# Fewer TensorE signals and fewer GpSimd waits in a two-layer graph network kernel

## The reference, cut to what matters

```
# layer 0
msgs   = x[dst] @ Wd + x[src] @ Ws + edge_weight[:, None] * ww + bm
agg    = segment_max(msgs, dst);  agg = where(deg > 0, agg, 0)
x1     = layernorm(x + relu(x @ W1a + agg @ W1b + b1) @ W2 + b2)
# layer 1
h      = x1 @ node_fc_W + node_fc_b
a      = sum(h[src] * h[dst], -1)                         # one number an edge
t      = relu((edge_attr @ edge_fc_W + edge_fc_b) @ rel_att_W1[m] + rel_att_b1[m])   # m = 0, 1, 2
g      = sigmoid(sum(t * rel_att_W2[m], -1) + rel_att_b2[m])
alpha  = segment_softmax(a, dst);  beta = segment_softmax(g, dst)
h_att  = segment_sum(alpha * (h[src] @ sum_k node_att_W[k])) / 3
h_rel  = segment_sum(sum_m beta[:, m] * (h[src] @ rel_att_W[m])) / 3
h_red  = relu(concat(h_att, h_rel) @ out_fc_W + out_fc_b)
out    = layernorm(x1 + gate * where(deg > 0, h_red, h) + (1 - gate) * x1)
```

## Time and profile before

| | |
|---|---|
| median of 3 runs | 2891.07 us (2887.76 to 2893.6) |
| the profiled execution | 2877.64 us, span 2875.9 us |
| busy share of the span | PE 65%, PEld 40%, DVE 46%, ACT 39%, POOL 59% |
| mean granted clock of TensorE | 0.786 of full speed |
| phase_runs, first to last gather | 73.7 to 1254.7 us |
| phase_nodes0, first gather to last product | 1291.9 to 1408.8 us |
| phase_edges, first gather to last window added | 1412.5 to 2745 us |
| gathers | 784 in phase_runs, 57 in phase_nodes0, 784 in phase_edges |

### The profile page before, as it was taken

One profiled execution on the slowest core, in us unless ns is written; L12 is line 12 of the kernel. 1 busy time (PEld: TensorE's weight loads), 2 busy tenths in 40 slices (PEclk: granted clock), 3 DMA queues, 4 the chain that ended last, 5 costly groups with the idle time before them and its releaser, 6 DMA issues. The chain is left out here.

```text
span 2875.9 us, 42972 instructions
## 1 busy us (share of the span) xinstructions
PE 1864.3 (65%) x9844; PEld 1144.2 (40%) x9844; DVE 1326.2 (46%) x5218; ACT 1107.7 (39%) x3259; POOL 1686.3 (59%) x1718
## 2 busy tenths in 40 slices
PE   4467777767667676455556666666666666666764
PEld 3112222222222222114445555555555555555663
DVE  3455444444433434323434444444444444444567
ACT  1133333333333333233454444444444444444533
POOL 1666666666776777636355555555555555555434
PEclk7688888888888888787767777778777777777786
DMA  5443333333333233322311121111111111111122
GB/s 179 153 177 104 119 105 119 104 119 104 119 103 99 100 115 114 106 75 81 108 44 51 46 51 49 48 49 51 45 51 50 47 49 51 49 47 51 46 68 69
DMA packets 115920, 238.36 MB, mean 83 GB/s; under 512 B 32905, under 2 KB 68422, under 8 KB 106102
## 3 DMA queue, kind: packets, MB, share of 16 engines
q0 software_dynamic: 52832, 109.39, 14.3%
q1 hardware_dynamic: 56458, 100.52, 9.5%
q10 hardware_dynamic: 6540, 27.42, 2.8%
HBM read 169.22 MB, written 67.89 MB: 82 GB/s over the span
## 5 line engine op out<-in xcount | busy, mean ns | idle before, releaser
L402 POOL DMA_INDIRECT d_region<-d_h,d_region x784 | 749.5, 956 | 556.0 <-issue 307.7
L515 POOL DMA_INDIRECT acc<-d_src_product,b_region x784 | 810.3, 1033 | 404.5 <-issue 215.3
L596 PE MATMUL banks<-acc,b_region 64*128 64x512 f32 x1176 | 367.5, 732 | 375.8 <-issue 166.5
L1500 DVE TENSOR_TENSOR acc<-acc,banks 128x160 f32 x784 | 252.6, 322 | 278.1 <-issue 82.8
L596 PEld LDWEIGHTS banks<-acc,b_region 64*128 64x128 f32 x1176 | 109.0, 211 | 583.4 <-issue 307.8
L804 DVE SCALAR_TENSOR_TENSOR acc<-b_region,acc 128x128 f32<-128x128 f32 x784 | 270.8, 346 | 124.7 <-DMA acc<-d_src_product,b_region 107.5
L701 ACT ACTIVATE gate_col<-banks,b_region 128x1024 f32<-128x1024 f32 x147 | 161.4, 1113 | 391.4 <-remote 273.9
L1296 PE MATMUL banks<-d_region 128*128 128x128 f32 x1568 | 297.5, 349 | 2.8 <-issue 2.5
L1299 PE MATMUL banks<-d_region,pick 128*128 128x128 f32 x1568 | 282.8, 338 | 6.1 <-issue 5.7
L815 DVE SCALAR_TENSOR_TENSOR acc<-acc,b_region 128x128 f32<-128x128 f32 x784 | 269.7, 344 | 29.3 <-remote 21.1
L1299 PEld LDWEIGHTS banks<-d_region,pick 128*128 128x128 f32 x1568 | 267.9, 255 | 8.4 <-issue 8.3
(11 more groups left out here) (259 smaller groups left out, 2467.4 us busy)
## 6 DMA issues: line engine op xcount, KB each, us to landing
d_runs<-acc SPq DMA_DIRECT2D x49, 1024.0 KB
acc<-ea ACTq DMA_DIRECT2D x25, 1024.0 KB
acc<-d_src_product,b_region POOLq DMA_INDIRECT x784
d_region<-d_rel SPq DMA_DIRECT2D x49, 256.0 KB
d_region<-d_h,d_region POOLq DMA_INDIRECT x784
acc<-xT SPq DMA_DIRECT2D x7, 448.0 KB, 5.5
d_src_product<-acc SPq DMA_DIRECT2D x7, 448.0 KB, 4.6
hT<-xT SPq DMA_DIRECT2D x1, 3136.0 KB
```

The source lines that it names most:

```text
L402: pool.indirect_dma_start(rows[:, s, :], None, table, bass.IndirectOffsetOnAxis(idx[:, s:s + 1], 0)).then_inc(gathered[q], 16)
L515: pool.indirect_dma_start(rows[:, s, j, :], None, d["B"], bass.IndirectOffsetOnAxis(idx[:, k:k + 1], 0)).then_inc(gat[s], 16)
L596: last = nc.tensor.matmul(bank[4 + n % 2 * 2 + h][:, :], wf[h * DE:(h + 1) * DE, m * P:(m + 1) * P], ea[h * DE:(h + 1) * DE, u % (2 * UC), ...
L1500: nc.vector.tensor_tensor(w, w, UZ[q % 2][:, :, j, :], ALU.add).then_inc(ad, 1)
```

## The change

1. **Edge pass, signals.** The five semaphores of TensorE become two. Its round is reordered to `turn_rows`, `spread`, `scores`, signal `m1`, `sums`, `turn_weights`, signal `m2`. Whoever waited for one of the five now waits for the signal of the half round that the operation lies in.
2. **Edge pass, order.** ScalarE does `rescale` first and `weigh` second in its round, `copy_weights` last. VectorE does `next_indices` first, then `references`, `lowest`, `picks`, `gate_weights` and `add_windows`.
3. **Edge pass, GpSimd.** The wait for turned rows (`tp`) goes. The wait for the sums becomes one for `m2`. The first lap is no longer written out apart.
4. **First message stage.** The signal of the third product of a unit goes (but for the first unit); ScalarE's third relu waits instead for the signal of the unit before, `dt`. The signal of `owner_rows` is merged into `dt`, which is given after both. So a unit has three signals instead of four or five. `has_edges` and the node part on VectorE move 3 and 4 groups later (`HAS_AT` 105 to 108, `PART_DVE` 108 to 112). GpSimd's wait for `dt` (the leash) goes.
5. **phase_nodes0.** GpSimd's wait for `ert` goes.

```diff
-def gather_rows(nc, pool, t, table, idx, rows, idx_ready, rows_used, rows_turned, gathered):
+def gather_rows(nc, pool, t, table, idx, rows, idx_ready, rows_used, gathered):
+    nit = iterations(pool, t)
+    def group(it, q):
+        pool.wait_ge(idx_ready, it * NG + (q + 1))
+        pool.wait_ge(rows_used, it * NG + (q + 2))
         hold(pool)
...
-    for q in range(NG):
-        group(0, q)
-    with pool.Fori(0, rest) as it:
+    with pool.Fori(0, nit) as it:
         for q in range(NG):
-            pool.wait_ge(rows_turned, it * NG + (NG + q - LAG + 1 + NG))
-            pool.wait_ge(idx_ready, it * NG + (NG + q + 1))
-            pool.wait_ge(rows_used, it * NG + (NG + q + 1))
-            gathers(q)
+            group(it, q)
...
-SHIFT_AT, HAS_AT = 100, 105
-PART_PE, PART_DVE, PART_STEP = 104, 108, 5
+SHIFT_AT, HAS_AT = 100, 108
+PART_PE, PART_DVE, PART_STEP = 104, 112, 5
...
+        def products_seen(u, m):
+            return m + 1 if u == 0 else M + (M - 1) * (u - 1) + m + 1
...
                 if g >= RG:
                     pool.wait_ge(ch, r_done(4 * (g - RG) + 3))
-                if g >= LEASH + 2:
-                    pool.wait_ge(dt, (g - LEASH) // 2)
...
-                    last.then_inc(tm, 1)
+                    if m < M - 1 or u == 0:
+                        last.then_inc(tm, 1)
...
-                    dots(g // 2)
-                b, off = divmod(g - SEL_AT, STEP)
-                if 0 <= b < NBLK and off == 0:
-                    owner_rows(b)
+                    last = dots(g // 2)
+                    if g // 2 < NBLK:
+                        last = owner_rows(g // 2)
+                    last.then_inc(dt, 1)
...
-                    act.wait_ge(tm, n + 1)
+                    if m < M - 1 or u == 0:
+                        act.wait_ge(tm, products_seen(u, m))
+                    else:
+                        act.wait_ge(dt, u)
...
-                    dve.wait_ge(sel, b - 1)
+                    dve.wait_ge(dt, b - 1)
...
-                dve.wait_ge(sel, b + 1)
+                dve.wait_ge(dt, b + 1)
...
             for b in range(NBLK):
-                if b % 4 == 0 and b // 4 >= 3:
-                    pool.wait_ge(ert, b // 4 - 2)
...
+        def in_round_of_rows(q):
+            return q - 4 + 5
+        def in_round_of_scores(q):
+            return q - 3 + 5
+        def in_round_of_bounds(q):
+            return q - 2 + 5
+        def in_round_of_weights(q):
+            return q - 1 + 2
+        def in_round_of_sums(q):
+            return q + 2
...
-            gather_rows(nc, pool, t, d["h"], idx, rows, idxr, ug, tp, gat)
+            gather_rows(nc, pool, t, d["h"], idx, rows, idxr, m2, gat)
...
             def group(it, q, end):
                 if q + 4 < end:
-                    turn_rows(it, q + 4)
+                    last = turn_rows(it, q + 4)
+                if 0 <= q + 2 < end:
+                    last = spread(it, q + 2)
                 if 0 <= q + 3 < end:
-                    scores(it, q + 3)
-                if 0 <= q + 2 < end:
-                    spread(it, q + 2)
+                    last = scores(it, q + 3)
+                if q + 2 < end:
+                    last.then_inc(m1, 1)
+                if q >= 0:
+                    last = sums(it, q)
                 if 0 <= q + 1 < end:
-                    turn_weights(it, q + 1)
-                if q >= 0:
-                    sums(it, q)
+                    last = turn_weights(it, q + 1)
+                if q >= -1:
+                    last.then_inc(m2, 1)
...
             def copy_rows(it, q):
-                act.wait_ge(tp, it * NG + (q + 1 + CREDIT))
-                act.wait_ge(sT, it * NG + (q - 2 + 1 + CREDIT))
+                act.wait_ge(m1, it * NG + (in_round_of_rows(q) + CREDIT))
...
             def copy_weights(it, q):
-                act.wait_ge(pt, it * NG + (q + 1 + CREDIT))
-                act.wait_ge(ug, it * NG + (q - 2 + 1 + CREDIT))
+                act.wait_ge(m2, it * NG + (in_round_of_weights(q) + CREDIT))
...
             def group(it, q, end):
+                if q >= 0:
+                    rescale(it, q)
                 if q + 4 < end:
                     copy_rows(it, q + 4)
+                if 0 <= q + 2 < end:
+                    weigh(it, q + 2)
+                if q + 4 < end:
                     windows(it, q + 4)
                     penalty(it, q + 4)
                 if 0 <= q + 3 < end:
                     link_values(it, q + 3)
                 if 0 <= q + 1 < end:
                     copy_weights(it, q + 1)
-                if q >= 0:
-                    rescale(it, q)
-                if 0 <= q + 2 < end:
-                    weigh(it, q + 2)
...
             def group(it, q, end):
+                if q % half == 0 and 0 <= q < end - NG:
+                    next_indices(it, q)
+                if 0 <= q + 2 < end:
+                    references(it, q + 2)
                 if 0 <= q + 3 < end:
                     lowest(it, q + 3)
                     picks(it, q + 3)
                 if 0 <= q + 1 < end:
                     gate_weights(it, q + 1)
-                if 0 <= q + 2 < end:
-                    references(it, q + 2)
-                if q % half == 0 and 0 <= q < end - NG:
-                    next_indices(it, q)
                 if q >= 0:
                     add_windows(it, q)
```

More of the change, by code:

```diff
@@ L403, in gathers @@
                                     bass.IndirectOffsetOnAxis(idx[:, s:s + 1], 0)).then_inc(gathered[q], 16)
-    for q in range(NG):
-        group(0, q)
-    with pool.Fori(0, rest) as it:
+    with pool.Fori(0, nit) as it:
         for q in range(NG):
-            pool.wait_ge(rows_turned, it * NG + (NG + q - LAG + 1 + NG))
-            pool.wait_ge(idx_ready, it * NG + (NG + q + 1))
-            pool.wait_ge(rows_used, it * NG + (NG + q + 1))
-            gathers(q)
+            group(it, q)
     for q in range(TAIL):
-        pool.wait_ge(idx_ready, rest * NG + (NG + q + 1))
-        pool.wait_ge(rows_used, rest * NG + (NG + q + 1))
-        gathers(q)
+        group(nit, q)
 RG = 6
-LAG = 4
 ST16 = 16
 HB = 3
-LEASH = 8
 NE = 8
@@ L443, in phase_runs @@
     with ExitStack() as ctx:
-        (ld, wld, pre, pre2, ch, ex, flg, hse, tm, ra, dt, gc, ohd, sel, cnt, has, fxi, fxd, enT, enc, enb,
+        (ld, wld, pre, pre2, ch, ex, flg, hse, tm, ra, dt, gc, ohd, cnt, has, fxi, fxd, enT, enc, enb,
          hr, hrc, gd, h1, h1c, h2, h2d, xbd, xl, owl, owp, owc, ows) = new_sems(*["b_" + n for n in (
                 "tables_loaded", "weights_loaded", "fold_product", "fold_copied", "chain", "extra_chain", "flag_rows",
-                "setup_done", "mlp_product", "relu_done", "dots_done", "gates_copied", "owner_marked",
-                "owner_rows", "owner_counted", "counts_shifted", "fix_index", "fix_done",
+                "setup_done", "mlp_product", "relu_done", "dots_and_owner_rows_done", "gates_copied", "owner_marked",
+                "owner_counted", "counts_shifted", "fix_index", "fix_done",
                 "end_turned", "end_scanned", "end_turned_back", "has_rows", "has_copied", "part_done", "hidden",
@@ L609, in dots @@
                                                 rt[u % 2][m][:, h * G4:(h + 1) * G4], start=(m == 0), stop=(m == M - 1))
-                last.then_inc(dt, 1)
+                return last
             def owner_rows(b):
@@ L617, in owner_rows @@
                 nc.tensor.matmul(bank[1][:, 0:EP // 2], oh[b % 2], dF[:, 0:EP // 2], start=True, stop=True)
-                nc.tensor.matmul(bank[2][:, 0:EP // 2 + 1], oh[b % 2], dF[:, EP // 2:EP + 1], start=True, stop=True
-                                 ).then_inc(sel, 1)
+                return nc.tensor.matmul(bank[2][:, 0:EP // 2 + 1], oh[b % 2], dF[:, EP // 2:EP + 1], start=True, stop=True)
             def hidden_out(c):
@@ L1265, in turn_rows, with spread @@
                     last = nc.tensor.transpose(TURNED[:, j * P:(j + 1) * P], rows[:, s * GJ + j, :], ident[:, :])
-                last.then_inc(tp, 1)
+                return last
+            def spread(it, q):
+                pe.wait_ge(mn, it * NG + (q + 1 + CREDIT))
+                pe.wait_ge(sl, it * NG + (q + 1 + CREDIT))
+                pe.wait_ge(rf, it * NG + (q - 1 + 1 + CREDIT))
+                return nc.tensor.matmul(BOUNDS[:, 0:8], vals[q % 2][:, 8:9].to_broadcast([P, P]), sel[q % 2][:, 0:8],
+                                        start=True, stop=True)
             def scores(it, q):
@@ L1274, in scores @@
                                             hs[q % 2][:, j * P:(j + 1) * P], start=True, stop=True)
-                last.then_inc(sT, 1)
-            def spread(it, q):
-                pe.wait_ge(mn, it * NG + (q + 1 + CREDIT))
-                pe.wait_ge(sl, it * NG + (q + 1 + CREDIT))
-                pe.wait_ge(rf, it * NG + (q - 1 + 1 + CREDIT))
-                nc.tensor.matmul(BOUNDS[:, 0:8], vals[q % 2][:, 8:9].to_broadcast([P, P]), sel[q % 2][:, 0:8],
```

(6 more changed lines are left out.)

40 lines of the change are left out of this document (19 added, 21 removed).

## The result

The changed kernel takes 3028.9 us (median of 4, 3020.56 to 3031.22) where the kernel before takes 2889.41: a ratio of 1.0492, 95% interval 1.0457 to 1.0527, 139 us slower. The forecast was slower, 2963 us in a range of 2770 to 3060. So sign and range held, and the size was half: +72 us forecast, +139 measured. Later the two kernels met chips on which the same comparison gives no difference; that is told with the experiments, and it is the larger find.

A forecast was written before the change was run, and what follows sets the result against it. It took GpSimd's pauses, waiting for TensorE signals held while it gathers, as the bound. Terms 3 + 25 + 0 + 34 + 0 + 10 + 0 = +72 us on 2891.07 gave 2963 us, range 2770 to 3060.

The forecast's parts named there:

- rest of phase_runs: After the 425th gather: 0 up to group 182, then the last 14 groups' gathers unbroken, -16 us.
- phase_nodes0: In phase_nodes0: 57 unbroken gathers, signals held to 5 us behind, then 12 steps at 4.0 us; +10, bounds -9 and +20.
- edge pass: Edge pass: removed turned-rows wait is implied by the sums' wait; merged m2 costs up to +60, runs of 8 save 30; taken 0.
- The reading of the trace: Whole kernel: TensorE signals given while GpSimd gathers without a pause are seen up to 20 us late; pauses let them through.
- Rival C: phase_runs and edge pass: fewer signals shorten the pauses, -34 and -49 us, 2808 us (2730 to 2880); chance 0.33.
- rival D: Late phase_runs: long gather runs also slow VectorE, 2.2 us for each of a group's 8 operations, 3130 us; chance 0.10.
- Up to the 425th gather: phase_runs up to group 105: VectorE's waits replace the leash three groups later, runs and pauses grow; +25 us, lower bound -88.
- the bound worked out for runs of 4 groups: phase_runs up to group 105: if runs stay 4 groups, 24 cycles with pauses 2.7 us longer give +66 us.
- The late stage: phase_runs, groups 105 to 182: VectorE's node-part waits replace the leash, longer runs with longer pauses; -36 to +36, taken 0.
- The tail: End of phase_runs: TensorE finishes 76 us after the last gather instead of 25.7, at 6.6 us a unit.
- the lower bounds together: Whole kernel: all terms' lower bounds added, given as -165 us.
- The count of signals: phase_runs and edge pass: 738 fewer signals taken as 0; the skill's 26.3 ns each would make -19 us (2872), chance 0.03.

The follow-up runs named there:

- run 6: Kernel before with only GpSimd's wait for dot products in phase_runs (the leash) removed, signals held: 2973.55 us against 2887.79, ratio 1.0292.
- run 8: Kernel before with only the edge pass of the kernel after, same chip as run 6: 2889.54 us against 2887.79, ratio 1.0024.
- Run 5: Kernel after, unchanged, on another chip where signals are seen at once: 2362.55 us against 2365.99 for the kernel before, ratio 0.9983.
- Run 7: Kernel after plus GpSimd memsets after every 16th gather of phase_runs and 8th of phase_nodes0, same chip as run 6: 2961.69 us, ratio 1.0259.

## Why the prediction was right in sign and short in size

Part by part, in us, with what run 6 (leash alone gone) takes more than run 8 on one chip:

| part | forecast | first two traces | run 6 less run 8 |
|---|---|---|---|
| first to 425th gather | +28 | +54.5 | +54.0 |
| rest of phase_runs | -16 | +25.7 | +3.1 |
| gap to phase_nodes0 | +50 | +38.5 | +24.0 |
| phase_nodes0 | +10 | +29.7 | +1.8 |
| edge pass | 0 | +6.0 | +1.1 |
| sum | +72 | +154.4 | +84.0 |

(Run 8 has the new edge pass, which is worth 0 within the noise.) So 84 of the 139 us are the leash's, shown on one chip. The other 55 or so were not taken apart while signals were held.

**The reading of the trace was right where it counts, and too narrow.** Run 5 and the first trace of the kernel after are the same code without and with held signals: with prompt signals phase_runs' gathers have no pauses, and the terms of the sum that rest on them are gone. Run 7 shows the other half, that in phase_nodes0 a gap of 2.0 us between gathers lets signals through even when GpSimd waits for no other engine. So the delay belongs to the gathers going on, not to a wait. Too narrow was "a signal of TensorE": VectorE's own come late as well, as its 35 waits for its own `step` show. Rival C (the number of signals matters) fell: the edge pass has two signals a round instead of five and takes 1295.2 against 1296.3 us on one chip. Of rival D the mechanism came and the price didn't. From 1294 to 1337 us VectorE does one `step` and `run` in 2.1 to 3.5 us, mostly 2.8, some 11 us a group (the forecast had a wait at each of the 8 operations, 20 us a group). But GpSimd stands only once for it, the 3.07 us before 1326.90, as the ring holds 6 groups: the last 56 gathers take 73.1 us, 5.2 a group. And VectorE is done at 1347.5, long before TensorE's last dot products at 1396.09, so no more of its lateness shows in the time.

**Up to the 425th gather: +25 (and +3 for the start) forecast, +54.5 measured.** This is the step that was mis-sized for a reason that the trace gives. I let runs grow to 5 or 6 groups with the longer lead, and named runs of 20 and more gathers as the sign of being right; they stayed 16 gathers and only the pause grew, from 3.65 to 5.9. The longer lead lengthened the first run alone; after it a cycle is still two of TensorE's units, and these are 4 groups. That is near the bound worked out for runs of 4 groups, +66. With the leash alone gone, run 6 gives 674.8 against 620.8 in run 8, the same 54: it is all the leash.

**The late stage: 0 forecast, +35 up to the 728th gather** (475.2 to 510.2 us) in the two first traces, then -9 where -16 was forecast. In the table this is the largest miss. On one chip, though, run 6 without the leash takes 582.7 for the whole second part and run 8 with it 579.6. The same code of phase_runs took 557.6 us there in the first trace and 579.6 in run 8, so how much of its term is the change's stays open.

**The tail: 76 us forecast, 64.5 measured,** against 25.7 before. Of these the leash makes most (run 6: the phase's gap is 62.3 us against 38.3 in run 8, +24). The rest goes with the slower unit, 6.52 us as forecast at 6.6, and with backlog: nine sets of dot products end behind the last gather, against eight in run 6. The 76 itself was the middle between two guesses of the backlog, 40 and 112, so that it came near is in part luck.

**phase_nodes0: +10 forecast, +20 its bound, +29.7 measured.** The gathers took the 71 us and the signals came 6.3 us behind them (ScalarE goes on at 1484.6), close to the 5 forecast. Wrong was what was left to do: from there to the last product (1553.5) it is 69 us, not 48. The last 12 steps lie 4.8 us apart (1492.63 to 1550.42), and the first had a whole chain of engines ahead of it. The edge pass' 4.0 us was a poor neighbour for a phase with other work; the earlier trace rows was of this phase, and I should have measured its steps. Run 7, with gaps between the gathers, is 28 us shorter in this phase. That the removed wait alone makes the +29.7 was not measured while signals were held.

**Edge pass: 0 forecast, +6.0 between the first traces, -1.1 on one chip (run 8 against run 6).** That fits the argument that the removed wait was implied. The bound beside it was off: runs of 8 throughout at 6.4 us a group are 1254 us, 50 less than 1304 and not 30, so the lower bounds together give -185.

**The count of signals.** The Trainium skill (TensorE: Matmul & The Clock Gate, "The cost: per-tile semaphore tail") prices an increment at 26.3 ns; 738 fewer would be an estimated 19 us. No run here shows it: with prompt signals the whole change is worth 0.17% (0.01 to 0.33), about 4 us and 8 at most, but there the gathers set the time and TensorE's savings lie beside them, so the rule is not tested by it.

**What stays open.** Why signals are held on one chip and not on another. Each chip stayed with its kind over all runs of the kernel before (17 at 2867.56 to 2912.8 us on the one, 61 at 2355.48 to 2375.81 on the three others), with the same instructions. The record does not name the chip of the first two traces, and each chip was met only once. Whether it is the chip, or something set when the program is placed on it, no run tells. The forecast holds only where signals are held: nothing in it says that on three of four chips the change makes no difference. Nor was any version found that beats the kernel before while signals are held.

## What to carry to other kernels

Before an order of waits is tuned, look how long after an instruction's end the one that waits for its signal starts, in a stretch where GpSimd issues indirect DMAs without a pause; if it is microseconds and ends when the gathers stop, then a wait of GpSimd that looks needless may be what lets the other engines go on, and what counts is who ends the pause. A leash must leave room for the distance at which the leashed engines are written to follow each other, or three engines wait in a ring (a leash of 4 against a `count` seven groups behind cost 18.6%). And compare kernels on the same chip, more than one: here a change is 4.9% slower on one and within 0.2% on another.

## What the runs showed of the hardware that was not expected

The same kernel takes 2889 us in one place and 2366 us on three chips, with the same instructions, and what differs is how soon signals are seen while GpSimd gathers without a pause: TensorE's 7.55 us late against 0.04 us in the rows shown, with waits of ScalarE of up to 43.0 us in phase_runs of the kernel after, and VectorE's `run` held 2.19 us by its own `step` against no such wait in 784 in run 5. A gap of 2.0 us between gathers, after a run of 8, let held signals through; of the 48 gaps of 1.4 us in phase_runs, after runs of up to 16, a held wait of ScalarE ended inside two. Since both the gap and the run differ, these do not give the width that it takes. TensorE's granted clock goes with it: 0.80 and 0.79 of full speed in phase_runs with held signals, 0.93 and 0.90 without, for the same products.
